# The opening of a graph, Performer and expert layer on Trainium2: pairs of tiles, and who splits V's first weights

## The reference

```python
xn = _layernorm(x, axis=-1)
x = x + gnn(xn, ...) + performer(xn[None], ...)[0]
# first lines of the Performer, per layer:
h = _layernorm(x, ln1_s[l], ln1_b[l])
q = heads(h @ Wq[l] + bq[l])
k = heads(h @ Wk[l] + bk[l])
v = heads(h @ Wv[l] + bv[l])
```

## Time and profile before

| what | value |
|---|---|
| median of 3 runs | 1143.89 us (1142.52 to 1146.07) |
| the profiled execution | 1144.43 us |
| its span | 1142.5 us |
| mean granted clock of TensorE in it | 0.991 |
| TensorE busy | 1086.5 us, 95% of the span |
| VectorE busy | 706.8 us, 62% |
| ScalarE, GpSimd busy | 365.4 us, 148.9 us |

### The profile page before, as it was taken

The page is one execution under the profiler, slowest core; times in us unless marked ns, Lnnn a source line. Parts: engine busy times, 40 slices in busy tenths (PEclk is TensorE's granted clock), DMA queues, the critical chain, the costliest instruction groups (busy, mean ns, idle before and its releaser), DMA issues.

```text
span 1142.5 us, 16284 instructions
## 1 busy us (share of the span) xinstructions
PE 1086.5 (95%) x6080; PEld 887.3 (78%) x6080; DVE 706.8 (62%) x1530; ACT 365.4 (32%) x671; POOL 148.9 (13%) x141
## 2 busy tenths in 40 slices
PE   7999899999999999999899999999999999999995
PEld 6767799878777777777798888777777888787763
DVE  7576677378766567465666469675563215834586
ACT  4335466525321211135466515221210002011231
POOL 4230202000000000300202000000000802200027
PEclk9999999999999999999999999999999999999998
DMA  6220101002222112000101003212156201100001
GB/s 212 111 93 1 38 1 39 1 5 83 82 53 78 53 50 79 1 1 1 38 2 38 1 5 97 88 48 64 56 193 229 94 20 38 36 1 1 1 10 65
DMA packets 34655, 60.17 MB, mean 53 GB/s; under 512 B 19441, under 2 KB 20401, under 8 KB 33937
## 3 DMA queue, kind: packets, MB, share of 16 engines
q1 hardware_dynamic: 12688, 41.21, 11.0%
q10 hardware_dynamic: 21888, 17.87, 4.9%
HBM read 48.59 MB, written 10.49 MB: 52 GB/s over the span
## 4 chain that ended last, share of the span: by engine, by line
PE 77%; DVE 10%; ACT 5%; issue 4%; POOL 3%; DMA 0%; POOLq 0%; ACTq 0%; DVEq 0%
PE ps_a L528 10%; PE ps_a L530 10%; PE ps_a L529 10%; PE ps_v L528 9%; PE ps_v L530 8%; PE ps_v L529 8%; PE ps_a L905 5%; PE ps_v L741 5%; PE ps_a L549 2%; PE ps_a L671 2%; PE ps_v L752 2%; ACT work L1090 2%; DVE expk L1556 2%; ACT expk L1051 1%; PE ps_v L625 1%
## 5 line engine op out<-in xcount | busy, mean ns | idle before, releaser
L528 PE MATMUL ps_a<-ht_hi,w_hi 128*128 128x512 f32 x488 | 193.7, 397 | 2.7 <-DVE w_lo L1822 0.9
L530 PE MATMUL ps_a<-ht_hi,w_lo 128*128 128x512 f32 x488 | 191.6, 393 | 0.0
L529 PE MATMUL ps_a<-ht_lo,w_hi 128*128 128x512 f32 x488 | 191.3, 392 | 0.0
L1001 ACT ACTIVATE work<-ps_a,col_sb 128x512 f32<-128x512 f32 x96 | 66.4, 719 | 198.7 <-PE ps_a L530 143.3
L528 PEld LDWEIGHTS ps_a<-ht_hi,w_hi 128*128 128x128 f32 x488 | 92.3, 189 | 25.7 <-DVE headmask_r L1521 1.3
L1675 DVE TENSOR_TENSOR xm<-ps_v,xm 128x512 f32<-128x512 f32 x80 | 55.2, 691 | 86.0 <-PE ps_v L530 85.3
L530 PEld LDWEIGHTS ps_a<-ht_hi,w_lo 128*128 128x128 f32 x488 | 92.3, 189 | 19.9
L529 PEld LDWEIGHTS ps_a<-ht_lo,w_hi 128*128 128x128 f32 x488 | 92.3, 189 | 19.3
L528 PE MATMUL ps_v<-w_hi,f_hi 128*128 128x512 f32 x256 | 101.7, 397 | 0.0
L530 PE MATMUL ps_v<-w_hi,f_lo 128*128 128x512 f32 x256 | 99.7, 389 | 0.0
L529 PE MATMUL ps_v<-w_lo,f_hi 128*128 128x512 f32 x256 | 99.6, 389 | 0.0
(11 more groups left out here) (240 smaller groups left out, 2016.8 us busy)
## 6 DMA issues: line engine op xcount, KB each, us to landing
stage<-wstream SPq DMA_DIRECT2D x62, 512.0 KB, 3.6
adj_d<-adj_win ACTq DMA_DIRECT2D x16, 256.0 KB, 2.9
adj<-adj_d ACTq DMA_DIRECT2D x2, 2048.0 KB, 11.9
xt_d<-xt_hi SPq DMA_DIRECT2D x2, 1024.0 KB, 5.0
xt_d<-xt_lo SPq DMA_DIRECT2D x1, 2048.0 KB, 11.4
ht_hi<-xt_d ACTq DMA_DIRECT2D x1, 2048.0 KB, 8.7
ht_lo<-xt_d ACTq DMA_DIRECT2D x1, 2048.0 KB, 13.4
x_again<-x ACTq DMA_DIRECT2D x8, 256.0 KB, 9.0
```

The costliest lines, as they stand in the source:

```text
L528: nc.tensor.matmul(ps, left[0], right[0], start=first, stop=False)
L529: nc.tensor.matmul(ps, left[0], right[1], start=False, stop=False)
L530: return nc.tensor.matmul(ps, left[1], right[0], start=False, stop=last)
L1001: nc.scalar.activation(work[:, n % 4, :], psA[:, i % BANKS, :], func, **how).then_inc(a_empty, 1)
```

## The change

x's tiles are announced in four pairs instead of two halves. VectorE takes statistics and aggregates for tiles 0 and 1 by itself, then for 2 and 3; GpSimd makes the deviation of each pair (`pair_deviation`, and `first_deviation` with other columns); VectorE normalises pair by pair. The statistics of tiles 4 and 5 stand behind that, those of 6 and 7 behind the four splits of half 0. V's low pieces stand between the splits (behind block 0 and block 1). TensorE waits block by block for V's tile 0, and most of its filling transposes are gone. V's high pieces are cast by GpSimd (`high_pieces`) between its first and second `first_deviation`. ScalarE gets a small activation that carries the table load, issues the loads of the projection and of the bias rows behind half 0's four copies, and makes the residual's rows behind the copies of both halves. GpSimd makes k's low weights only when half 1 is split.

```diff
-        x_in = [sem("x_in0"), sem("x_in1")]
+        x_in = [sem("x_in0"), sem("x_in1"), sem("x_in2"), sem("x_in3")]
...
-            keep_busy(8, var_ready, 1)
-            keep_busy(8, rstd_ready, 1)
+            keep_busy(8, first_rstd, 1)
...
-                    keep_busy(16)
-                    for j in range(PIECES):
-                        keep_busy(8, w_split, j + 1)
-                    for k in range(KT - 1):
-                        keep_busy(8, split, done(MIX_SPLIT["n1", 0, k]))
-                slot = weight_slot("v")
+                    keep_busy(8)
+                    keep_busy(8, split, done(MIX_SPLIT["n1", 0, 0]))
+                def first_block(k):
+                    pe.wait_ge(w_split, k // 2 + 1)
+                    need_split(("n1", 0, k))
+
+                slot = slot_of(SLOT_OF["v"]) if L == 0 else weight_slot("v")
                 for t in range(NT):
+                    if L == 0 and t == 0:
+                        into_nat(slot, hT, t, bank("v", ("v", t)), first_block).then_inc(v_full, 1)
+                        continue
...
-            high_weight(0, SLOT_OF["v"])
-            load_proj(0)
-            load_rows(0)
+            act.wait_ge(p_chain, 1)
+            nc.scalar.activation(rden[:, 0, 0, :], nhalf[:, 0:2], ACT.Copy)
...
                     if L == 0 and name == N1_ORDER[KT - 1]:
+                        act.wait_ge(w_in[1], 16)
+                        load_proj(0)
+                        load_rows(0)
+                        act.wait_ge(w_split, PIECES)
                         high_weight(1, SLOT_OF["k"])
-                        act.wait_ge(rstd_x_ready, 1)
-                        for t in range(NT):
-                            nc.scalar.activation(Xm[:, t, :], nat[:, t, :], ACT.Identity, scale=rstd_x[:, t:t + 1],
-                                                 bias=shift_x[:, t:t + 1]).then_inc(x_normed, 1)
+                if L == 0:
+                    act.wait_ge(rstd_x_ready, 1)
+                    for t in range(NT):
+                        nc.scalar.activation(Xm[:, t, :], nat[:, t, :], ACT.Identity, scale=rstd_x[:, t:t + 1],
+                                             bias=shift_x[:, t:t + 1]).then_inc(x_normed, 1)
...
+            def high_pieces():
+                for j in range(PIECES):
+                    pool.wait_ge(w_in[j], 16)
+                    nc.gpsimd.tensor_copy(Whi[:, SLOT_OF["v"], 2 * j:2 * j + 2, :].rearrange("p a b -> p (a b)"),
+                                          stage[:, j, :]).then_inc(w_high, 1)
+
+            pair_deviation()
             first_deviation(0)
+            high_pieces()
             first_deviation(1)
...
-            pool.wait_ge(split, done(MIX_SPLIT[N1_ORDER[KT - 1]]))
+            pool.wait_ge(split, done(MIX_SPLIT[N1_ORDER[-1]]))
             low_weight(1, SLOT_OF["k"])
-            pool.wait_ge(split, done(MIX_SPLIT[N1_ORDER[-1]]))
             split_weight(2, SLOT_OF["q"])
...
-            for h in range(H):
-                dve.wait_ge(x_in[h], 64)
-                statistics(loaded, half_tiles(h))
-                aggregate(half_tiles(h), h + 1)
-                if h == 0:
-                    normalise_half(loaded, nat1, normed, 0)
-            low_weight(0, SLOT_OF["v"])
+            def low_piece(j):
+                hi, lo = (w[:, SLOT_OF["v"], 2 * j:2 * j + 2, :].rearrange("p a b -> p (a b)") for w in (Whi, Wlo))
+                dve.wait_ge(w_high, j + 1)
+                nc.vector.tensor_tensor(lo, stage[:, j, :], hi.bitcast(f32), ALU.subtract).then_inc(w_split, 1)
...
+            dve.wait_ge(x_in[0], 32)
+            for t in range(2):
+                last = nc.vector.bn_stats(stats[:, t, :], loaded(t))
+            last.then_inc(first_stats, 1)
+            dve.wait_ge(first_stats, 1)
+            for t in range(2):
+                last = nc.vector.bn_aggr(mv[:, t, :], stats[:, t, :])
+            last.then_inc(first_var, 1)
+            dve.wait_ge(x_in[1], 32)
+            statistics(loaded, range(2, 4))
+            aggregate(range(2, 4), 1)
+            dve.wait_ge(first_rstd, 1)
+            normalise_pair(0)
+            dve.wait_ge(rstd_ready, 1)
+            normalise_pair(1)
+            dve.wait_ge(x_in[2], 32)
+            statistics(loaded, range(4, 6))
...
                     for k in range(KT):
                         split_t(("n1", 0, k), hT, k, 0)
+                        if k < PIECES:
+                            low_piece(k)
+                    dve.wait_ge(x_in[3], 32)
+                    statistics(loaded, range(6, NT))
+                    aggregate(half_tiles(1), 2)
                 normalise_half(loaded if L == 0 else residual, nat1, normed, 1, L * 4, LN_FIRST)
```

28 lines of the change are left out of this document (18 added, 10 removed).

## The result

Over 15 executions the changed kernel takes 1139.85 us (median), the kernel before 1144.62 over 15 of its own. The ratio is 0.9951, with a 95% interval of 0.9934 to 0.9967, so the gain is 5.6 us and lies between 3.8 and 7.6. One execution of the changed kernel, at 2751.03 us, was disturbed and is left out of the ratio. A second series of 12 executions gave 1139.83 us and a ratio of 0.9966 (0.9945 to 0.9988). 1140.0 was predicted.

A forecast was written before the change was run, and what follows sets the result against it. TensorE, busy for 95% of the span, was taken to bound the kernel, so the opening's 4.1 us would stay: 1144.43 - 4.1 = 1140.3, or 1139.8 from the median. It predicted 1140.0 us, range 1137.9 to 1142.6.

The forecast's parts named there:

- The statistics in pairs: Opening, VectorE and GpSimd: pair 0 normalised from 7.7 to 8.7, the fourth tile ready between 10.45 and 12.05 us.
- TensorE's own start: Opening: 24 filling transposes at 1.2 GHz end at 11.45, so half 0's turn starts between 11.45 and 12.05 us.
- The term right behind it: From half 0's turn to its first copy: 0.64 us, plus 0.05 for a clock that may still be rising.
- The pieced block: V's first tile, started block by block behind the splits: half 1's turn at 26.25 us, a gain of 4.1 us.
- Half 1 in time: Half 1's four normalisations end at 25.2 to 26.0, before its turn, with 0.2 to 1 us to spare.
- the rival that gave them 6.1 for it: Half 1's normalisations, slowed beside GpSimd's eight-column operations, take 6.1 us; gain only 0.9 us, 1143.5 us; chance 7%.
- The moved rest, at nothing: Residual rows, k's weights and loads, moved later on ScalarE and GpSimd, delay nothing; cost 0 us.
- ScalarE becomes the bound: Residual rows on ScalarE delay the residual's turn by up to 5.7 us; 1146.0 us; chance 4%.
- The sum: Whole kernel: the opening's 4.1 us off 1144.43 gives 1140.3, or 1139.8 from the median; 1140.0 predicted.
- The last rival: Opening: half 0's turn stays at 12.6, the pieced block alone gives 3.4 us; 1141.0 us, counted within the forecast's 69%.
- The rivals on the clock: TensorE's clock level falls in V's pieced first block, costing about 1.6 us; 1141.9 us; chance 20%.
- gone at the end: Sign that the prediction is wrong: the 4 us are there at 50 us but gone at the kernel's end.

The follow-up runs named there:

- e1_four: The changed kernel, but VectorE's first statistics wait until the tiles of both first pairs have landed; 1143.57 us in one execution.
- e10_after_again: The changed kernel once more with no new edit, timed; median 1139.83 us over 12 executions, ratio to the kernel before 0.9966.
- e3_low_k_early: The changed kernel with GpSimd making k's low weights behind half 0's splits again, not half 1's; 1145.03 us in one execution.
- e4_rows_early: The changed kernel with the residual's eight rows on ScalarE ahead of half 1's copies again; 1148.12 us in one execution.
- e5_before_low_k_late: The kernel before with one edit, GpSimd's low weights of k moved behind half 1's splits; 1141.96 us in one execution.

## Why the prediction was right

**The statistics in pairs.** The power on two columns took 0.72 (predicted 0.9, between half of 1.05 and all of it). Pair 0 was normalised from 7.35 to 8.32 (7.7 to 8.7), and the fourth tile was ready at 9.92, earlier than both ends of my range (10.45 to 12.05). The range's upper end was a real event, only not of this kernel: e1_four shows it at 12.74. I had pair 1's deviation ready between 9.4 and 10.1, and it was there at 8.88, early enough for VectorE to be done 0.45 ahead of GpSimd's cast.

**TensorE's own start.** "The turn starts between 11.45 and 12.05": 11.61. The term right behind it was under-sized. I added 0.05 to the 0.64 from turn to copy for a clock that may still be rising; it was 1.02, since the level rose in the midst of the turn. The two misses, 0.3 early and 0.33 late, cancel, and that is luck: cast 0 at 13.44 against 13.4. In e10_after_again, with the level up at 10.54, it is at 12.45.

**The pieced block.** Last split 20.06 (20.0), V's block 0 at 15.83 (15.8), block 3 at 20.20 (20.1), turn of half 1 at 26.42 (26.25), V's tile 4 at 32.27 (32.1). The durations of the kernel before carried over unchanged, and TensorE's idle times in front of blocks 1 and 2 are 0.17 and 1.27; in front of block 3, where I had named a gap too, the timeline shows none.

**Half 1 in time.** Normalised at 25.22 (25.2 to 26.0), with 1.2 us to spare. VectorE waited 0.17 for the copy; I had it ready 0.2 behind the copy. The four took 1.92, though GpSimd's eight-column power for the residual (23.97 to 25.82) ran beside them, and the rival that gave them 6.1 for it is out. e3_low_k_early shows the same port contention one step further on, at the casts.

**The moved rest, at nothing.** k's high weights were done at 23.75 (24.6 at the latest), the residual's rows ran from 29.72 to 35.47 (29.7 to 35.4), k's low weights from 32.30 to 37.05. "ScalarE becomes the bound" did not happen, but its margin was the 0.30 that ScalarE still waits. e4_rows_early shows the price when these rows do stand in the way: 5.0 us.

**The sum.** Minus 4.1 was predicted for the opening, 3.94 measured in the profiled pair, up to 4.9 where the level rises as early as in e10_after_again. The median fell by 4.8, the ratio says 5.6 with 3.8 to 7.6 around it. The 1.7 us between opening and ratio lie within that interval and are no finding.

**The last rival.** I gave the change behind an unmoved turn 3.4 us, and called that the pieced block alone. e1_four, with its turn at 12.80, shows 3.0 for all of it; the pieces alone are 2.0 of the 3.94, by the table. That the pairs, V's low pieces between the splits and the later statistics share the rest in some way was not taken apart: no run has the pairs without VectorE's new order, and only e1_four comes near to the order without the pairs.

**The rivals on the clock, and "gone at the end".** The level did not fall in the pieced block, in any of the eleven profiles that have it. It did fall at 34 to 35 in e3_low_k_early and e4_rows_early, behind idle time of TensorE of some microseconds. The price that I gave such a stretch on dense work, 1.6, is of the right size: the jumps of the lead in the profiled pair are 1.0 to 1.9. It isn't the price of every one: over the 14 profiles a stretch goes with 0.72 more, as the end of this paragraph shows. The sign that I named against myself, 4 us at 50 us and less at the end, did half appear, 2.0 left of 3.9. It was the wrong sign to name: with two to eight low stretches in an execution, two profiles alone differ by as much as that. Over the 14 profiles the rest behind the head mask follows 1087.2 us plus 0.72 for each low stretch, with a spread of 1.1 us. The changed kernel's two profiles stand 1.3 above and 1.5 below that line, the kernel before's 0.8 above it, so nothing behind the opening tells them apart.

## What to carry to other kernels

When a start is brought forward, take the works it will newly run beside (here k's low weights on GpSimd and the residual's rows on ScalarE) out of its way in the same step: both were hidden before, and they cost 3 and 5 us when left where they were. Moving the first one alone gained nothing (0.12 us); the second wasn't tried alone. A fast path of several engines is set by the one whose queue is fixed in time, here TensorE's 24 fillings until 11.6; winning more on the others buys mainly distance from collisions. With the fillings fewer, V's high weights, which can't be cast before they land, take that place, on GpSimd until 12.5 or on ScalarE until 11.5. And judge an edit of 1 us at the marks of its own stage over several profiles, since the whole program's time varies by more for reasons that lie elsewhere.

## What the runs showed of the hardware

- A power on GpSimd is mostly fixed cost: in the profiles before and after two columns take 0.72 and 0.88 us, four 1.01 and 1.04, eight 1.85 and 2.12. Another power on four columns in the kernel before, beside VectorE's subtractions for V's low weights, took 1.87.
- When TensorE's level first rises varies from execution to execution with much the same work ahead of it: between 9.25 and 12.27 us in 14 profiles, all of which start the same transposes at 5.8 to 6.5. It moved the opening of the changed kernel by 1 us, and that of e5_before_low_k_late, with the earliest rise, by only 0.12 against the kernel before.
- A VectorE instruction that meets GpSimd's cast or subtraction lasts about until that one is over, also where it is much shorter itself: a cast of 0.43 took 1.26 beside a GpSimd cast of 1.04 that had started 0.06 earlier, and a subtraction of 0.69 took 2.77.
- Stretches of 3.4 us at 1.2 GHz come two to eight times in an execution behind the head mask, near places that recur but not each time. They cost 1.0 to 1.9 us each where they could be read singly, and 0.72 on average over the 14 profiles.
